# Second-phase projections as three float32r products of rounded parts and residues

## The reference

```python
def _layer(x, wqkv, qs, ksc, wo, lg, lb, w1, b1, w2, b2):
    h = shift_token(x)                    # second half of the channels comes from the token before
    q, k, v = jnp.split(h @ wqkv, 3, axis=-1)
    ...
    q = l2norm(q) * qs
    k = l2norm(k) * ksc
    q, k = rotary_xpos(q, k)
    o = local_attention(q, k, v)          # window of 128 tokens and the window before
    x = x + o.transpose(0, 2, 1, 3).reshape(b, n, INNER) @ wo
    h = shift_token(x)
    h = (h - mu) / jnp.sqrt(var + 1e-05) * lg + lb
    a, g = jnp.split(h @ w1 + b1, 2, axis=-1)
    h = a * jax.nn.gelu(g, approximate=False)
    return x + h @ w2 + b2
```

## Time and profile before

| what | value |
| --- | --- |
| median of 3 runs | 5642.62 us (5640.09 to 5645.47) |
| profiled execution | 5642.98 us |
| its span | 5641.2 us |
| mean granted TensorE clock | 0.992 |
| PE busy | 5465.1 us, 97% of the span |
| DVE busy | 4151.5 us, 74% |
| ACT busy | 3453.4 us, 61% |
| POOL busy | 970.1 us, 17% |
| chain that ended last, by engine | PE 71%, ACT 11%, issue 10%, DVE 4%, POOL 3% |

### The profile page before, as it was taken

One profiled execution on the slowest core, in us unless ns is written; L12 is line 12 of the kernel. 1 busy time (PEld: TensorE's weight loads), 2 busy tenths in 40 slices (PEclk: granted clock), 3 DMA queues, 4 the chain that ended last, 5 costly groups with the idle time before them and its releaser, 6 DMA issues.

```text
span 5641.2 us, 145376 instructions
## 1 busy us (share of the span) xinstructions
PE 5465.1 (97%) x57552; PEld 2666.8 (47%) x57552; DVE 4151.5 (74%) x10780; ACT 3453.4 (61%) x6979; POOL 970.1 (17%) x1933
## 2 busy tenths in 40 slices
PE   8999999999999999999799999999999999999998
PEld 3444444444444444533455555555555555555553
DVE  5888888787888888787566667666666777677774
ACT  4766667676666767666455555555556565555654
POOL 2222222232222223222000000000000001010100
PEclk9999999999999999999899999999999999999998
DMA  3333333233333333333100000000000000000000
GB/s 70 55 55 69 55 60 60 50 74 55 66 55 59 63 51 72 55 60 76 43 12 16 8 16 12 12 16 8 16 32 19 16 19 16 20 16 20 19 16 19
DMA packets 128518, 215.60 MB, mean 38 GB/s; under 512 B 40032, under 2 KB 40160, under 8 KB 127072
## 3 DMA queue, kind: packets, MB, share of 16 engines
q1 hardware_dynamic: 127840, 206.30, 18.1%
HBM read 45.73 MB, written 25.17 MB: 13 GB/s over the span
## 4 chain that ended last, share of the span: by engine, by line
PE 71%; ACT 11%; issue 10%; DVE 4%; POOL 3%; SPq 0%; DMA 0%; POOLq 0%; ACTq 0%; DVEq 0%
PE ps L573 22%; PE ps L698 14%; PE ps L819 10%; PE ps L1040 6%; PE ps L1003 5%; PE ps L904 3%; ACT pt L1257 3%; PE ps L896 3%; PE ps L921 3%; ACT gates L1455 1%; ACT sm L1374 1%; PE ps L1005 1%; PE ps L871 1%; PE ps L880 1%; POOL both L2119 1%
## 5 line engine op out<-in xcount | busy, mean ns | idle before, releaser
L1257 ACT ACTIVATE pt<-ps 128x1024 f32<-128x1024 f32 (+7 forms) x2048 | 1237.5, 654 | 616.2 <-PE ps L573 465.1
L698 PE MATMUL ps<-pt,va 128*32 128x512 f32 (+3 forms) x3072 | 1226.5, 487 | 20.0 <-POOL pt L2089 20.0
L698 PE MATMUL ps<-pt,ones 128*32 128x512 f32 (+3 forms) x6144 | 1236.4, 489 | 0.0
L698 PE MATMUL ps<-pt,vs 128*32 128x512 f32 (+3 forms) x3072 | 1230.1, 488 | 0.0
L1631 DVE CUSTOM_DVE_ANT_0 junk<-ps,causal 128x128 bf16<-128x128 f32 (+3 forms) x2048 | 977.8, 487 | 298.4 <-PE ps L573 282.1
L573 PE MATMUL ps<-kt,qt 96*32 96x512 bf16 (+3 forms) x12288 | 1018.6, 329 | 43.8 <-DVE mc L1631 22.7
L573 PE MATMUL ps<-qt,kt 98*32 98x512 bf16 (+3 forms) x12288 | 835.9, 328 | 21.9 <-ACT pt L1257 21.0
L1635 DVE TENSOR_REDUCE mc<-ps 128x1 f32<-128x512 f32 x1024 | 706.4, 690 | 158.7 <-PE ps L573 127.9
L2089 POOL TENSOR_SCALAR_AFFINE_SELECT pt<-pt 128x256 f32<-128x256 f32 x1024 | 466.8, 456 | 1892.2 <-ACT pt L1257 1890.4
L819 PE MATMUL ps<-wqkv,xs 128*128 128x512 f32 x1536 | 727.9, 603 | 0.0
L1374 ACT ACTIVATE sm<-sm,mxw 128x256 f32<-128x256 f32 (+1 forms) x1024 | 493.5, 484 | 241.0 <-DVE mxw L1800 239.6
(11 more groups left out here) (151 smaller groups left out, 8551.3 us busy)
## 6 DMA issues: line engine op xcount, KB each, us to landing
qt<-part SPq DMA_DIRECT2D x768, 64.0 KB, 2.4
kt<-part SPq DMA_DIRECT2D x768, 64.0 KB, 2.5
ya<-wy SPq DMA_DIRECT2D x128, 128.0 KB, 2.3
yb<-wy SPq DMA_DIRECT2D x128, 128.0 KB, 2.3
xs<-between_phases SPq DMA_DIRECT2D x32, 512.0 KB, 3.8
xt<-in_x SPq DMA_DIRECT2D x16, 512.0 KB, 5.6
between_phases<-z SPq DMA_DIRECT2D x16, 512.0 KB, 2.8
between_phases<-xo SPq DMA_DIRECT2D x16, 512.0 KB, 2.7
```

Source lines behind the costliest of these rows:

```text
L698: mmi = pe.matmul(ps[32 * q:32 * q + 32, 4 + half, lo - half * 512:hi - half * 512], w, probs(kb)[:, i, lo - first(kb):hi - first(kb)], st ...
L1257: act.activation(probs(kb)[:, i, kb * P - first(kb):1024 - first(kb)], ps[:, 2 * i:2 * i + 2, :].rearrange("p a q -> p (a q)")[:, kb * P:1 ...
```

## The change

Every projection of the second phase is computed as three float32r matmuls in place of one float32 matmul. An operand is split into a rounded part (the same number cast to float32r) and a residue (the number less its rounded part); the three products are rounded by rounded, and the two of a rounded part with a residue. The product of the two residues is left out. Every other step computes what it did.

```diff
+PRODUCTS = (((0, 0, 0, 0), (0, 0, 1, 1), (0, 1, 0, 2)), ((0, 1, 1, 3), (1, 0, 0, 4), (1, 0, 1, 5)))
+THREE = ((0, 0), (1, 0), (0, 1))
...
-            def project(W, n, bank, kc):
-
-                w, l = W % WIN, W // (nb * WIN)
-                at = w * P + 1 - kc
-                return pe.matmul(ps[:, bank, :], xs[:, kc, at:at + P], wqkv[l][:, kc, n * 512:n * 512 + 512],
-                                 start=kc == 0, stop=kc == 1)
+            def project(W, n, bank, part_of):
+
+                w = W % WIN
+                for x, y, kc, k in PRODUCTS[part_of]:
+                    at = w * P + 1 - kc
+                    mmi = pe.matmul(ps[:, bank, :], (xsh, xsl)[x][:, kc, at:at + P], (wh, wl)[y][:, kc, n * 512:n * 512 + 512],
+                                    start=k == 0, stop=k == 5)
+                return mmi
...
                 for f in fs:
-                    mmi = pe.matmul(ps[:, fbank(m, 1 + oc), :], wo[:, f, oc * P:(oc + 1) * P],
-                                    ot[:, f, half * 512:half * 512 + 512], start=f == 0, stop=f == 3)
+                    for k, (x, y) in enumerate(THREE):
+                        mmi = pe.matmul(ps[:, fbank(m, 1 + oc), :], (woh, wol)[x][:, f, oc * P:(oc + 1) * P],
+                                        (oth, otl)[y][:, f, :], start=f == 0 and k == 0, stop=f == 3 and k == 2)
...
                 for j in js:
...
+                    if oc == 0:
+                        pe.wait_ge(hhl_done, done(m * HB + j + 1))
...
                 act.wait_ge(fn_done, done(m + 1))
                 for kc in range(2):
+                    act.activation(cnh[:, kc, :], cn[:, kc, :], ACT.Identity,
+                                   scale=lnp[:, 0, kc:kc + 1], bias=lnp[:, 1, kc:kc + 1]).then_inc(cnh_done, 1)
                     act.activation(cn[:, kc, :], cn[:, kc, :], ACT.Identity,
                                    scale=lnp[:, 0, kc:kc + 1], bias=lnp[:, 1, kc:kc + 1]).then_inc(hn_done, 1)
...
+            def split_wqkv(n, lo, hi):
+                pool.wait_ge(wq_ready, sent(1 + n))
+                pool.tensor_copy(wh[:, :, lo:hi], wraw[:, :, lo:hi]).then_inc(wqh_done, 1)
+                pool.wait_ge(wqh_done, done(1 + n))
+                pool.tensor_tensor(wl[:, :, lo:hi], wraw[:, :, lo:hi], wh[:, :, lo:hi], ALU.subtract).then_inc(wql_done, 1)
...
+            def residue(m):
...
+                for kc in range(2):
+                    pool.wait_ge(cnh_done, done(2 * m + kc + 1))
+                    pool.wait_ge(hn_done, done(2 * m + kc + 1))
+                    pool.tensor_tensor(cnl[:, kc, :], cn[:, kc, :], cnh[:, kc, :], ALU.subtract).then_inc(cnl_done, 1)
...
+            def attend(W):
+                m, c = half_of(W), W % 4
+                if c == 0:
+                    combine(W + 1)
+                    final_channels(m - 1)
+                    if m >= 0:
+                        sum_channels(m)
+                        sum_squares(m)
+                    split_heads(W)
+                elif c == 1:
+                    residue(m)
+                    combine(W + 1)
+                    split_x(W // WIN + W % WIN // 4, 1 - W % WIN // 4)
+                    final_sum_squares(m - 1)
+                    split_heads(W)
+                elif c == 2:
+                    combine(W + 1)
+                    for j in range(HB - 1):
+                        split_hidden(m, j)
+                    split_heads(W)
+                    split_hidden(m, HB - 1)
+                else:
+                    combine(W + 1)
+                    split_heads(W)
...
+                if W % (4 * FIRST) == 3:
+                    split_wo(W // (4 * FIRST))
+                    split_w1(W // (4 * FIRST))
+                if W % (4 * FIRST) == 6:
+                    split_w2(W // (4 * FIRST))
+                if W == 4 * FIRST - 2:
+                    split_wqkv(1, 0, 1024)
+                if W == 4 * FIRST - 1:
+                    split_wqkv(2, 1024, 1536)
```

More of the change, by code:

```diff
@@ L8 @@
 BF16 = mybir.dt.bfloat16
+F32R = mybir.dt.float32r
 ALU = mybir.AluOpType
@@ L153, in sb, with over @@
             top[0] = at + n
+            place[name] = at
             return nc.alloc_sbuf_tensor_at(name, shape, dt, offset=at)
+        def over(name, other, shape, dt):
+            return nc.alloc_sbuf_tensor_at(name, shape, dt, offset=place[other])
         def sem(name):
@@ L316, in program @@
         stored = [sem(f"stored{h}") for h in range(2)]
-        wq_ready = [sem(f"wq_ready{l}") for l in range(LAYERS)]
+        wq_ready = sem("wq_ready")
         wo_ready = sem("wo_ready")
@@ L363, in program @@
         hn_done = sem("hn_done")
+        cnh_done = sem("cnh_done")
+        cnl_done = sem("cnl_done")
+        w1h_done = sem("w1h_done")
+        w1l_done = sem("w1l_done")
+        w2h_done = sem("w2h_done")
+        w2l_done = sem("w2l_done")
+        woh_done = sem("woh_done")
+        wol_done = sem("wol_done")
+        wqh_done = sem("wqh_done")
+        wql_done = sem("wql_done")
+        xsh_done = [sem(f"xsh_done{h}") for h in range(2)]
+        xsl_done = [sem(f"xsl_done{h}") for h in range(2)]
+        xm_ready = [sem(f"xm_ready{h}") for h in range(2)]
+        oth_done = sem("oth_done")
+        otl_done = sem("otl_done")
+        hhh_done = sem("hhh_done")
+        hhl_done = sem("hhl_done")
         g_full = sem("g_full")
@@ L978, in final_variance, with normed @@
                 pe.wait_ge(lc_done, done(n + 1))
-                pe.matmul(ps[:, 6, :], mean_w[:], bothf[:, 1, :], start=True, stop=True).then_inc(lvar_full, 1)
+                pe.matmul(ps[:, 6, :], mean_w[:], sqx[:, 0, :], start=True, stop=True).then_inc(lvar_full, 1)
+            def normed(m, n, to, tile, width, parts):
+                for part_of in parts:
+                    if n == 0 and part_of == 1:
+                        pe.wait_ge(cnl_done, done(2 * m + 2))
+                    for x, y, kc, k in PRODUCTS[part_of]:
+                        mmi = pe.matmul(to, (w1h, w1l)[y][:, kc, tile, 0:width], (cnh, cnl)[x][:, kc, :],
+                                        start=k == 0, stop=k == 5)
+                return mmi
             def gate(m, j, beside, kcs=(0, 1)):
@@ L1024, in hidden @@
                     pe.wait_ge(hh_done, done(m * HB + j - 1))
-                for kc in kcs:
-                    mmi = pe.matmul(ps[:, fbank(m, 13 + j), :], w1[:, kc, HB - 1 + j, :], cn[:, kc, :], start=kc == 0, stop=kc == 1)
+                mmi = normed(m, HB + j, ps[:, fbank(m, 13 + j), :], HB - 1 + j, P, kcs)
                 if kcs[-1] == 1:
@@ L1039, in ffn_out @@
                     rows = slice(0, P if j < HB - 1 else HLAST)
-                    mmi = pe.matmul(ps[:, fbank(m, 19 + oc), :], w2[rows, j, oc * P:(oc + 1) * P], hh[rows, j, :],
-                                    start=j == 0, stop=j == HB - 1)
+                    if oc == 0:
+                        pe.wait_ge(hhl_done, done(m * HB + j + 1))
+                    for k, (x, y) in enumerate(THREE):
+                        mmi = pe.matmul(ps[:, fbank(m, 19 + oc), :], (w2h, w2l)[x][rows, j, oc * P:(oc + 1) * P],
+                                        (hhh, hhl)[y][rows, j, :], start=j == 0 and k == 0, stop=j == HB - 1 and k == 2)
                 if js[-1] == HB - 1:
@@ L2134, in final_sum_squares, with split_w1 @@
                 pool.wait_ge(lvar_full, done(n))
[L2135 removed]
+                pool.tensor_tensor(sqx[:, 0, :], sqx[:, 0, :], sqx[:, 1, :], ALU.add).then_inc(lqc_sum, 1)
+            def split_w1(l):
+                pool.wait_ge(w1_ready, sent(l + 1))
+                for kc in range(2):
+                    pool.tensor_copy(w1h[:, kc, :, :], w1[:, kc, :, :]).then_inc(w1h_done, 1)
+                for kc in range(2):
+                    pool.wait_ge(w1h_done, done(2 * l + kc + 1))
+                    pool.tensor_tensor(w1l[:, kc, :, :], w1[:, kc, :, :], w1h[:, kc, :, :], ALU.subtract).then_inc(w1l_done, 1)
@@ L2156, in _ @@
             sum_squares(m)
+            residue(m)
+            for j in range(HB):
+                split_hidden(m, j)
             final_channels(m)
```

225 lines of the change are left out of this document (149 added, 76 removed).

## The result

The changed kernel takes 5666.2 us (median of 5 runs, 5664.1 to 5669.1), 1.0043 times the kernel before, with a 95% interval of 1.0028 to 1.0057: slower by 0.4%, inside the predicted range, but 64 us short of the predicted 5730. The span of the profiled execution grew from 5641.2 to 5662.4 us, by 21.2.

The account below looks back on a forecast made before the run. The prediction took TensorE and the rotation chain to be in balance, with little slack. From 5643 us, windows -10, lower clock +64 and one-offs +33 gave 5730 us; range 5550 to 5850.

Parts of the forecast that it names:

- What the waiting does to the clock: Second phase: TensorE's longer waits lower its granted clock, losing 2.0 us a half (bounds nothing and 5.1), +64 us.
- three waits of two us or more: TensorE was expected to wait about this often per half, in windows c = 1, 2 and 3.
- The slack bounds the gain: Before transpose_q: the rotation chain leaves TensorE 3.4 us of slack a half; time saved beyond it becomes waiting.
- The windows: A half's four windows, c = 0 to 3: -0.75 us a half in layer 1, +0.15 in layer 2, -10 us in all.
- three blocks of 0.5 us: Window c = 2: GpSimd's hidden-tile splits hold up VectorE's two-SBUF-input operations, 0.5 us each, counted as 1.4 us.
- GpSimd's prices: A split on GpSimd: a subtraction of 1.28 us and a cast of 0.62, 1.9 us.
- TensorE's step: A float32r projection matmul takes 0.216 us, against 0.43 for a float32 record, saving 14.0 us a half.
- One-offs: Weight splits at the turns of layers and phases and before the first feed-forward products: 11 + 12 + 7 + 3 = +33 us.
- The sum: Whole kernel: 5643 - 10 + 64 + 33 = 5730 us.
- (a): Rival: GpSimd's work misses VectorE's SBUF steps and lost clock is absorbed, so windows gain their slack; about 5560 us, chance 0.27.
- (b): Rival: float32r matmuls stream at the float32 record's 0.43 us, so TensorE bounds again; about 6550 us, chance 0.10.
- (c): Rival: TensorE's saving of 448 us falls out in full; 5228 us, chance 0.03.

Follow-up runs that it names:

- one_product: Changed kernel with only the rounded-by-rounded product of the three kept, all splits and waits staying: 5742.8 us, 1.0182 times the kernel before.
- early_exp: gate_order's edit on the changed kernel, plus ScalarE's last exponentials ahead of the first two gate results in c = 1 windows: 5659.8 us, 1.0034 times the kernel before.
- late_hidden: Changed kernel with GpSimd waiting for the next window's rotation to end before splitting the hidden tile: 5680.5 us, 1.0071 times the kernel before.
- gate_order: Changed kernel with the first three matmuls of the gate's second block before the second three of its first: 5660.9 us, 1.0035 times the kernel before.
- no_residue: Changed kernel with GpSimd's four kinds of activation subtractions cut to 16 columns each, TensorE's matmuls as many: 5538.6 us, 0.9820 times the kernel before.
- two_product: Changed kernel with the product with the input's residue left out, all splits and waits staying: 5664.2 us, 1.0041 times the kernel before.
- heads_act: Changed kernel with the heads split by a ScalarE cast and a VectorE subtraction from PSUM, without GpSimd: 5637.7 us, 0.9991 times the kernel before.

## Why the prediction was off

The step that failed is "What the waiting does to the clock": **+64 us** became about 8. The mechanism is real (one_product), but its size hung on "three waits of two us or more" a half, and the trace has 7 such waits in all, none of them in an ordinary half. Two reasons show. TensorE's idle time is 285 / 31 = 9.2 us a half and not 14: a step is 0.23 us, not 0.216, and the first float32r matmul behind transposes takes 0.32 (5043.06 to 5043.38, at L1117). And it falls into four or five pieces of about 1.1 us, since each engine's list has other steps between the waits. In most halves the clock holds through these pieces. A half of layer 1 in which it does not:

```profile
3548.48 0.70 PE L1054 MATMUL ps<-cnh,w1h 128*128 128x512 f32 x2 [1.01 <-ACT cnh L1489]
...
3550.80 0.80 PE L1054 MATMUL ps<-cnh,w1l 128*128 128x512 f32 x1 [1.38 <-POOL cnl L2273]
3551.39 1.06 PE L1054 MATMUL ps<-cnl,w1h 128*128 128x512 f32 x2
3552.24 1.06 PE L1054 MATMUL ps<-cnh,w1h 128*128 128x512 f32 x2
```

```profile
3540.00:3560.00 20.00, 17.08 (x69) 12.26 (x68) 13.46 (x32) 14.71 (x34) 10.71 (x11) 0.83 0.09 28
4980.00:5000.00 20.00, 18.20 (x110) 12.50 (x111) 14.82 (x32) 14.35 (x32) 10.79 (x12) 1.00 0.09 27
```

Two matmuls take 0.85 us from start to start (3552.24 - 3551.39), and the granted clock of the stretch is 0.83. In the half of layer 2 shown further up the second wait is 1.09 us, but the first only 0.18; the same two matmuls take 0.46 us (4997.01 - 4996.55), and the granted clock is 1.00. The 14 halves of layer 1 from window 9 to 61 all have both waits, of 1.01 to 1.04 and of 1.09 to 1.38 us. In six of them the lower clock follows, and the interval of c = 1 is 26.0 to 27.9 us; in the other eight it is 25.06 to 25.41. The six lose 8.0 us against these: that is what became of the +64. From window 73 on, in layer 2, the first wait is under 0.3 us, and no window with c = 1 loses clock. As a check from the other side, a clock of 0.99 over 2726 us is 27 us of TensorE's work lost, where 5.1 us in each of 31 halves would make 158; some 12 of the 27 lie in those six windows, the rest around the one-offs, in whose prices it is counted.

The row on which I had priced the term was of a wait of 2.00 us, and the mistake was to treat all of TensorE's expected idle time as pieces of that kind without walking one half's list and placing each piece. That many short pieces cost less than few long ones of the same sum is what these rows suggest; no run holds the sum fixed and changes the length alone.

The other steps, one by one:

- *The slack bounds the gain:* right. TensorE's work fell by 8.7 us a half, (2707 - 2438) / 31, and a half became 0.3 us (layer 1) and 0.6 us (layer 2) shorter.
- *The windows.* Change of the interval, mean over layer 1: c = 0 -1.86 (predicted -1.6), c = 1 +1.94, or +1.43 without the lower clock (+1.3), c = 2 +0.07 (+0.55), c = 3 -0.49 (-1.0). In layer 2: -1.10 (-0.7), +0.59 (+1.3), +0.37 (+0.55), -0.49 (-1.0). None is off by more than about 0.7 us; without the lower clock a half became 0.85 us (layer 1) and 0.63 us (layer 2) shorter, where -0.75 and +0.15 had been forecast. Two slips in the working make 0.3 us a half, some 10 us: three blocks of 0.5 us are 1.5 and not 1.4, and 1.8 us with a block are 2.3 and not 2.1. A single block is larger than the 0.5 us that I counted, up to 1.1 (2.29 - 1.22) here and 2.0 in early_exp, but fewer fall on the chain. The Trainium skill's rule of exclusion for the whole instruction ("SBUF — State Buffer", on who interferes with whom) is closer to these rows than my 0.5.
- *GpSimd's prices:* cast 0.61 us (0.62 taken), subtraction 1.27 (1.28). *TensorE's step:* 0.23 (0.216 taken; the row itself says 0.22).
- *One-offs:* 11 at the turn of the layers was 12.5, 12.31 of it one wait of the queries; 9.5 a layer for the other weights was some 12 to 13; the turn of the phases is -2.0 in this trace where +3 was counted, but it is +1.7 to +2.2 in those of late_hidden, gate_order and early_exp, whose work is the same up to window 4, so it is not told from nothing. Together 12.5 + 11.7 + 12.9 - 2.0 = 35, predicted 33.
- *The sum:* 5643 - 10 + 33 = 5666 without the clock, which is the measured time to less than a microsecond; that is luck in part, since the halves gave some 24 us and not 10, the lower clock took about 8 of it back, and the 35 us of one-offs contain a start that differs by 4 us between traces.
- *Rivals:* (a) was nearly right on the clock and wrong on the blocks, which no_residue prices at 128 us, the gate's wait for the residue included. (b) is excluded by the 0.23 us. The estimate of 0.43 us from the Trainium skill's figure ("SBUF — State Buffer"), which the page gives for bf16, does not hold for this matmul; the row decides. (c) is excluded by the 97.6 us before `transpose_q`, and by two_product, in which 308 us less of work bring nothing.

What stays open: why the two waits of about 1 us before the gate are followed by the lower clock in six halves of layer 1 and not in the other eight.

## What to carry to other kernels

A TensorE that is 97% busy may still have only tenths of a microsecond of slack against the chain beside it: before work is taken from it, look at how late its inputs are at each wait, since beyond that slack the gain is nothing, and with more and longer idle time, as in one_product, it can be less than nothing. Work handed to an idle GpSimd is not free where VectorE's operations have two SBUF inputs: a cast on ScalarE and a subtraction on VectorE that reads PSUM did the same split of the heads with fewer blocks (heads_act, 28.5 us). When a clock penalty is priced, place each wait in the engine's list first: here 9 pieces over 1.5 us went with a granted clock of 0.99, 120 with 0.94 and 252 with 0.80 (285, 593 and 826 us of idle time in all).

## What had not been expected of the hardware

Fewer matmuls made the kernel slower: one product instead of three took 2437.92 - 1895.89 = 542 us off TensorE's busy time in the steady stretch, and added 77 us to the kernel, at a granted clock of 0.80. A float32r matmul of 128x512 has a step of 0.23 us, close to the 0.22 between the groups of bf16 matmuls in the earlier trace rows and about half of the 0.43 of one float32 record; its weight load of 128x128 takes 0.19 (mean of PEld at L883), so it is just hidden. GpSimd's casts, with one input, wait for VectorE's operations with two SBUF inputs too: 1.07 us instead of 0.61.
